# A bidirectional Mamba block with a gated feed-forward layer: the decay ring carried over the chunks, and Silu, evacuations, output products and a norm at other steps

## Chip, cores and metric

The kernel runs on one core of a Trainium2 chip. The metric is the device time of one execution in microseconds (us), the median of a few runs. The core has five engines with queues of their own: PE (TensorE, matrix products), DVE (VectorE), ACT (ScalarE), POOL (GpSimd) and SP, which here only issues DMAs. Each engine takes its instructions strictly in the order in which they are written; engines meet through semaphores.

## The reference

Input x has shape (2, 4096, 256). The network normalises and modulates x, runs a Mamba block over it forwards and backwards in time, joins the two, and adds a feed-forward part. All of the change lies in the Mamba block, whose core is this:

```python
xi = silu(conv(in_proj_x(x)))              # 512 channels, causal convolution over 4 tokens
dt, Bm, Cm = split(xi @ x_proj.T)          # dt: 64 -> 512 channels; B and C: 16 states
dt = softplus(dt @ dt_w.T + dt_b)
dA  = exp(dt[..., None] * A)               # the decay, 512 channels x 16 states
dBx = (dt * xi)[..., None] * Bm[:, :, None, :]
h_t = dA_t * h_(t-1) + dBx_t               # the scan over time
y_t = sum_s(h_t * C_t) + xi * D
out = (y * silu(z)) @ out_proj.T           # z is the other half of in_proj
```

## The kernel before

**Tiling.** Time is cut into chunks of T = 512 tokens. There are 2 passes (backwards, then forwards), 8 chunks per pass and batch entry, and 2 batch entries, which take turns: 32 chunks in all, called chunk 0 to 31 below (0 to 15 are pass 0). Channels lie on the 128 partitions, in KI = 4 groups. A chunk has 16 states x 4 groups = 64 scans of 128x512, the steps 0 to 63. Two steps are a unit: units 0 to 31, each of one state and of two channel groups. `half` 0 is units 0 to 15 and half 1 is units 16 to 31.

**What happens in a step.** ACT computes the decay of step k (`decay`, L885) into one of NDA = 3 banks of PSUM, the decay ring. DVE scans it (`scan`, L1057). POOL multiplies dt*xi by B for both groups of a unit (`weigh_b`, L968) into one of four buffers `dBx`. Four units later the states `h` of a unit are multiplied by C: on DVE for 23 of the 32 units (`D_UNITS`, L1066, with C spread over the partitions by PE, L663), on POOL for 9 (`P_UNITS`, L979). Before that ACT copies the last column of each pair of units as the state for the next chunk (`keep_state`, L829). PE turns the weighed states and sums them in PSUM (L681); after 16 units it adds the skip part (L693) and ACT evacuates the sum (`evacuate`, L849). A chunk ends in gates with silu(z) (DVE, L1045) and the output product (PE, L648), evacuated by ACT with Tanh (L861).

**Order.** Chunk n's scans run beside the front part of chunk n+1 (turn of the normalised x, in_proj, convolution, x_proj, dt, z), the tail of chunk n-1 (last gates, output product) and, in pass 0, the norm of x for chunk n+2. Nothing is scheduled by a program. Tuples by hand say at which step each job starts on PE (`AT`); ACT follows PE's table `ACT_LAG` = 3 steps later, and other tuples name the steps of jobs that are ACT's alone. ACT's body is

```python
for k in range(STEPS):
    decay(ch, k)
    if k == EVAC[1] and has(ch, -1): evacuate(ch.go(-1), 1)
    if k == EVAC[0]: evacuate(ch, 0)
    tail(ch.go(-1), k)
    front(ch.go(1), k); xi_silu(ch.go(1), k)
    z_silu(ch, k)
    scale_skip(ch, k)
    if k % 4 == 2: keep_state(...)         # units (k-6)/2 and (k-6)/2 + 1
    if k == AT_XN and norms(ch, 2): norm_x(ch.go(2))
```

ACT's functions need tables: Silu is in one set, Exp in another, so each group of Silu has an ACT_TABLE_LOAD before it and one behind it, before the next decay. Copies and Identity need no load.

**The decay ring.** `decay(k)` waits until the bank's last user has been scanned. Before the change the banks are fixed per chunk, `SLOT = [k % 3 for k in 0..62] + [1]`: decay k waits for scan k-3, except that decay 63 waits for scan 61 and decay 1 for scan 63 of the chunk before.

Of the kernel before, what the change touches and what calls it, by code (L numbers as in the profile page):

```python
# [22 lines left out]
KI = DI // P  # L23
# [17 lines left out]
AT = {J_LN: (0, 1), J_X: (3, 5, 7, 9), J_CONV: (11, 16, 20, 24), J_DT: (35, 40, 43, 49), J_Z: (50, 52, 54, 56),  # L41
      J_Y: (46, 47, 13, 17), J_OUT: (33, 39)}
AT_LN, AT_X, AT_CONV, AT_DT, AT_Z, AT_Y, AT_OUT = (AT[j] for j in (J_LN, J_X, J_CONV, J_DT, J_Z, J_Y, J_OUT))
# [9 lines left out]
NDA = 3  # L53
SLOT = [k % NDA for k in range(STEPS - 1)] + [1]
NH, NDBX = 8, 4
# [4 lines left out]
ACT_LAG, DVE_LAG = 3, 2  # L60
EVAC = (43, 11)
AT_XI, AT_ZS = (24, 24, 31, 31), (20, 20, 62, 62)
AT_XN = 27
AT_EXP = (48, 53)
AT_LNP = (49, 54)
NORM_STAT, NORM_AGGR, RSTD_S = 6, 7, 11
AT_XD = (14, 15, 16, 18)
# [7 lines left out]
RAW_ROWS = 128  # L75


def since_slot(k):

    return next(n for n in range(1, STEPS) if SLOT[(k - n) % STEPS] == SLOT[k])  # L80

# [242 lines left out]
def mamba(nc, a, bank, ident, cols, mod, norm_c, x_v, yb_v, yf_v, xn_v, b_dram, c_dram, w_raw, s_raw, S):  # L324
# [10 lines left out]
    with ExitStack() as c:  # L335
# [219 lines left out]
        def _(pe):  # L555
# [15 lines left out]
            def front(ch, g):  # L571
# [10 lines left out]
                for m in range(KI):  # L582
# [27 lines left out]
                    if g == AT_B + m:  # L610

                        pe.wait_ge(S["xi"], ch.at(KI, m + 1))
                        part(ch, J_B, m, KI, w_x[:, m, :], xi[:, m, :], B0 + 2 * DS)
# [120 lines left out]
        def _(act):  # L734
# [70 lines left out]
            def xi_silu(ch, g):  # L805
                for m in range(KI):
                    if g == AT_XI[m]:
                        if m == 0:

                            wait(act, S["u_ready"], ch.at(2, 0))  # L810
                        wait_drained(act, ch, J_CONV[m])
                        act.activation(xi[:, m, :], u[:, ch.batch, m, :], ACT.Silu).then_inc(S["xi"], 1)

            def scale_skip(ch, g):
                for m in range(KI):
                    if g == AT_XD[m]:
                        if m == 0:
                            act.wait_ge(S["xi"], ch.at(KI, KI))
                            act.sem_inc(S["go"], 1)
                            wait(act, S["y_turned"], ch.at(2, 0))  # L820
                        col = COL_D + m
                        act.activation(xD[:, m, :], xi[:, m, :], ACT.Copy, scale=cols[:, ch.ps, col:col + 1]
                                       ).then_inc(S["skip"], 1)
# [8 lines left out]
            def z_silu(ch, g):  # L832
                for m in range(KI):
                    if g == AT_ZS[m]:
                        wait_drained(act, ch, J_Z[m])
                        o = z[:, ch.batch, m, :]
                        act.activation(o, o, ACT.Silu).then_inc(S["z"], 1)
# [38 lines left out]
            def decay(ch, k):  # L876
# [148 lines left out]
        def _(dve):  # L1025
# [502 lines left out]
```

## Time and profile before

| | us |
|---|---|
| median of 3 runs (lowest, highest) | 5023.15 (5022.44, 5025.08) |
| the profiled execution | 5024.78, with a span of 5023.0 |
| busy over the span: PE, DVE | 4351.3, 4014.6 |
| busy over the span: ACT, POOL | 3278.4, 3469.0 |

The span is what the core's instructions take; the 1.8 us more of the profiled execution lie around it. The scans run from 156.7 to 3608.2 us of the span, the feed-forward part after that. In the profile a row of a timeline gives the start, the length, the engine, the line, the operation and how many like it follow each other; behind it in brackets stands the idle time of the engine before it, and what ended that.

### The profile page before, as it was taken

To read this page: it belongs to the slowest core of one execution; us is meant where nothing else is said; L and a number is where in the kernel's file an instruction comes from. 1 tells how busy PE (TensorE), PEld (TensorE's weight loads), DVE (VectorE), ACT (ScalarE), POOL (GpSimd) and SP (SyncE) were. 2 spreads that over 40 slices of the span, in tenths; PEclk is the share of its full clock that TensorE was granted. 3 is DMA by queue.
4 is the path that set the end of the run, shared out by engine and by line. 5 is a ranking of instruction groups with operands and counts; after the bars stand their busy time and mean duration, and the time that the engine had idled before them with its cause. 6 is when DMAs were issued, how large, how long until landed. Compare 5 with 4: busy or idle time off the path is not lost. (4 is left out here: it accounts for less than half of the span.)

```text
span 5023.0 us, 61527 instructions
## 1 busy us (share of the span) xinstructions
PE 4351.3 (87%) x22474; PEld 3152.1 (63%) x22474; DVE 4014.6 (80%) x4232; ACT 3278.4 (65%) x5347; POOL 3469.0 (69%) x1589
## 2 busy tenths in 40 slices
PE   3788888888888888888888888888679999999999
PEld 2455555555555655555555555655568888888887
DVE  4699999999999999999999999999744444444442
ACT  4777777777777777777777777777434444444443
POOL 4899999999999999999999999999600000000000
PEclk7999999999999999999999999999889999999999
DMA  4533333333333333333333333323231010101000
GB/s 141 196 116 118 112 112 120 117 116 110 110 112 112 123 115 113 117 111 111 115 106 115 112 110 114 111 110 106 75 132 35 28 36 27 37 26 38 26 30 9
DMA packets 175537, 474.42 MB, mean 94 GB/s; under 512 B 14912, under 2 KB 99264, under 8 KB 140608
## 3 DMA queue, kind: packets, MB, share of 16 engines
q1 hardware_dynamic: 174336, 458.92, 26.6%
q10 hardware_dynamic: 896, 11.54, 0.7%
q8 instruction: 179, 2.93, 0.2%
q14 instruction: 126, 1.03, 0.1%
HBM read 434.75 MB, written 47.19 MB: 96 GB/s over the span
## 5 line engine op out<-in xcount | busy, mean ns | idle before, releaser
L968 POOL TENSOR_TENSOR m_dBx<-m_u,m_Bs 128x1024 f32<-128x1024 f32 x1024 | 2398.7, 2369 | 38.6 <-DVE m_h L1057 34.1
L1057 DVE TENSOR_TENSOR_SCAN m_h<-bank,m_state,m_dBx 128x512 f32<-128x512 f32 x1792 | 2185.5, 1264 | 90.9 <-ACT bank L885 87.7
L885 ACT ACTIVATE bank<-m_dt,cols 128x512 f32<-128x512 f32 x2048 | 1382.7, 690 | 514.9 <-DVE m_h L1057 510.9
L681 PEld LDWEIGHTS bank<-ident,m_h 128*128 128x128 f32 x8192 | 1013.3, 147 | 665.2 <-issue 331.8
L681 PE MATMUL bank<-ident,m_h 128*128 128x128 f32 x8192 | 1260.3, 284 | 155.3 <-DVE m_h L1066 134.8
L1066 DVE TENSOR_TENSOR m_h<-m_h,bank 128x1024 f32<-128x1024 f32 x736 | 879.9, 1196 | 12.1 <-PE bank L663 11.3
L663 PEld LDWEIGHTS bank<-ident,m_Ct 128*128 128x128 f32 x2944 | 345.3, 143 | 728.3 <-DVE m_h L1066 521.3
L663 PE MATMUL bank<-ident,m_Ct 128*128 128x128 f32 x2944 | 485.1, 290 | 365.9 <-DVE m_h L1066 364.7
L1339 POOL TENSOR_TENSOR mvj<-mvj,norm_c 128x4 f32<-128x4 f32 x16 | 16.2, 1013 | 1098.8 <-DVE mvj L1389 1098.8
L979 POOL TENSOR_TENSOR m_h<-m_h,m_Cs 128x1024 f32<-128x1024 f32 x288 | 683.0, 2371 | 30.4 <-ACT m_state L829 26.7
L567 PE MATMUL bank<-m_hT,m_w_in 128*128 128x512 f32 x1024 | 549.9, 623 | 12.8 <-ACT m_hT L755 12.8
L567 PE MATMUL bank<-m_xpre,m_diag 128*128 128x512 f32 x1024 | 522.8, 595 | 0.0
L1227 PE MATMUL bank<-gb,h 128*128 128x512 f32 x2048 | 481.6, 396 | 0.0
L1227 PE MATMUL bank<-ga,h 128*128 128x512 f32 x2048 | 480.5, 396 | 0.0
L1227 PEld LDWEIGHTS bank<-ga,h 128*128 128x128 f32 x2048 | 384.7, 188 | 93.1
L1227 PEld LDWEIGHTS bank<-gb,h 128*128 128x128 f32 x2048 | 383.6, 188 | 91.7
L1431 DVE TENSOR_TENSOR ga<-raw,ga 128x512 fp32r<-128x512 f32 x256 | 176.1, 688 | 315.8 <-ACT raw L1299 314.3
L1057 DVE TENSOR_TENSOR_SCAN m_h<-bank,m_dBx 128x512 f32<-128x512 f32 x256 | 297.6, 1205 | 77.6 <-ACT bank L885 69.7
L1431 DVE TENSOR_TENSOR gb<-raw,gb 128x512 fp32r<-128x512 f32 x128 | 88.7, 693 | 245.0 <-ACT raw L1299 245.0
L1297 ACT ACTIVATE gb<-bank,fcol 128x512 fp32r<-128x512 f32 x128 | 88.2, 689 | 291.6 <-PE bank L1227 291.6
L1297 ACT ACTIVATE ga<-bank,fcol 128x512 fp32r<-128x512 f32 x128 | 88.2, 689 | 288.3 <-PE bank L1227 288.3
L648 PE MATMUL bank<-m_w_out,m_z 128*128 128x256 f32 x1024 | 263.8, 381 | 1.9 <-DVE m_z L1045 1.1
(125 smaller groups left out, 4919.8 us busy)
## 6 DMA issues: line engine op xcount, KB each, us to landing
m_Bs<-b_dram SPq DMA_DIRECT2D x256, 1024.0 KB, 4.7
m_Cs<-c_dram SPq DMA_DIRECT2D x288, 256.0 KB, 3.2
m_xy<-in_x SPq DMA_DIRECT2D x16, 512.0 KB, 7.1
xn_dram<-m_xn SPq DMA_DIRECT2D x16, 512.0 KB, 4.5
yb_dram<-m_ysb SPq DMA_DIRECT2D x16, 512.0 KB, 2.9
m_xn<-xn_dram SPq DMA_DIRECT2D x16, 512.0 KB, 3.8
x_dram<-m_ysb SPq DMA_DIRECT2D x16, 512.0 KB, 2.9
x<-x_dram SPq DMA_DIRECT2D x16, 512.0 KB, 5.0
```

Of the source, the lines that this page charges most:

```text
L567: mm = pe.matmul(FB[BANK[i]][0:rows, :], lhsT, rhs, start=(k == 0), stop=(k == kn - 1))
L648: mm = pe.matmul(FB[BANK[J_OUT[i]]][:, (r // 2) * DM:(r // 2 + 1) * DM], z[:, q, k, s * P:(s + 1) * P], w_out[:, k, :], start=(k == 0), st ...
L663: mm = pe.matmul(CB[:, t * P:(t + 1) * P], Ct[:, ch.batch, t, s:s + 1].broadcast_to((P, P)), ident[:, :], start=True, stop=True, is_transp ...
L681: mm = pe.matmul(YB[b][:, o:o + P], h[:, k % NH, m, tok:tok + P], ident[:, :], start=(s == 0 and o == 0), stop=False, is_transpose=True, s ...
L885: act.activation(DA[SLOT[k]][:, :], dt[:, ch.batch, m, :], ACT.Exp, scale=cols[:, ch.ps, col:col + 1]).then_inc(S["da"], 1)
L968: pool.tensor_tensor(dBx[:, k % NDBX, :, :], u[:, ch.batch, m, :], Bs[:, k // BP % 2, k % BP, :].unsqueeze(1).broadcast_to((P, 2, T)), ALU ...
L979: pool.tensor_tensor(o, o, Cs[:, i % 2, :].unsqueeze(1).broadcast_to((P, 2, T)), ALU.mult).then_inc(S["weigh_p"], 1)
L1057: dve.tensor_tensor_scan(h[:, k % NH, m, flip(ch)], DA[SLOT[i]][:, flip(ch)], dBx[:, k % NDBX, m, flip(ch)], initial, ALU.mult, ALU.add).t ...
L1066: dve.tensor_tensor(o, o, CB[:, :].unsqueeze(1).broadcast_to((P, 2, T)), ALU.mult).then_inc(S["weigh_d"], 1)
L1227: return pe.matmul(out, lhsT, rhs, start=start, stop=stop)
L1297: act.activation(dst, bank[b][:, :], func, **args).then_inc(S["hi"], 1)
L1431: dve.tensor_tensor(dst[:, 1], raw[:, j % XR, :], dst[:, 0].bitcast(F32), ALU.subtract).then_inc(S["lo"], 1)
```

## The change

The ring goes on over the chunks: the bank of a decay is its number since the start of the kernel modulo 3, and each decay waits for the scan three before it. Both Silu of xi in a half become one instruction of 128x1024, and so do those of z. The Silu of z for half 0 moves from step 20 to step 5. The evacuations move from steps 43 and 11 to 44 and 12. The output products start on PE at steps 29 and 35 in place of 33 and 39, so their Tanh on ACT come at 35 and 41 in place of 39 and 45. The norm of x is applied on ACT at step 19 in place of 27; its statistics on DVE move from units 6 and 7 to 4 and 5, its four small operations on POOL from unit 11 to 8.

```diff
--- before.py
+++ after.py
@@ -39,7 +39,7 @@
 J_LN, J_X, J_CONV, J_B, J_DT, J_Z = (0, 1), (2, 3, 4, 5), (6, 7, 8, 9), 10, (11, 12, 13, 14), (15, 16, 17, 18)
 J_Y, J_OUT, J_C = (19, 20, 21, 22), (23, 24), 25
 AT = {J_LN: (0, 1), J_X: (3, 5, 7, 9), J_CONV: (11, 16, 20, 24), J_DT: (35, 40, 43, 49), J_Z: (50, 52, 54, 56),
-      J_Y: (46, 47, 13, 17), J_OUT: (33, 39)}
+      J_Y: (46, 47, 13, 17), J_OUT: (29, 35)}
 AT_LN, AT_X, AT_CONV, AT_DT, AT_Z, AT_Y, AT_OUT = (AT[j] for j in (J_LN, J_X, J_CONV, J_DT, J_Z, J_Y, J_OUT))
 AT_B, AT_C = 29, 37
 NFB = 2
@@ -51,19 +51,18 @@
 
 
 NDA = 3
-SLOT = [k % NDA for k in range(STEPS - 1)] + [1]
 NH, NDBX = 8, 4
 W_LAG, T_LAG = 4, 5
 P_UNITS = (1, 5, 7, 9, 13, 15, 17, 21, 25)
 D_UNITS = tuple(k for k in range(NU) if k not in P_UNITS)
 ND, NP = len(D_UNITS), len(P_UNITS)
 ACT_LAG, DVE_LAG = 3, 2
-EVAC = (43, 11)
-AT_XI, AT_ZS = (24, 24, 31, 31), (20, 20, 62, 62)
-AT_XN = 27
+EVAC = (44, 12)
+AT_XI, AT_ZS = (24, 31), (5, 62)
+AT_XN = 19
 AT_EXP = (48, 53)
 AT_LNP = (49, 54)
-NORM_STAT, NORM_AGGR, RSTD_S = 6, 7, 11
+NORM_STAT, NORM_AGGR, RSTD_S = 4, 5, 8
 AT_XD = (14, 15, 16, 18)
 ADD_S = (27, 2)
 U_S = (31, 6)
@@ -73,11 +72,6 @@
 FFN_WEIGHTS = ("w1T", "w2T", "h1T", "h2T", "w3T")
 PIECE, RING = 2 * DH, 4
 RAW_ROWS = 128
-
-
-def since_slot(k):
-
-    return next(n for n in range(1, STEPS) if SLOT[(k - n) % STEPS] == SLOT[k])
 
 
 class Chunk:
@@ -609,7 +603,7 @@
                         part(ch, J_Z[m], k, KM, w_in[:, k, (KI + m) * P:(KI + m + 1) * P], hT[:, k, :])
                     if g == AT_B + m:
 
-                        pe.wait_ge(S["xi"], ch.at(KI, m + 1))
+                        pe.wait_ge(S["xi"], ch.at(2, m // 2 + 1))
                         part(ch, J_B, m, KI, w_x[:, m, :], xi[:, m, :], B0 + 2 * DS)
                 if g == AT_C:
                     rows = B0 + 2 * DS
@@ -803,19 +797,21 @@
                         act.activation(dt[:, q, m, :], FB[b][:, :], ACT.Relu, bias=bias).then_inc(drain[b], 1)
 
             def xi_silu(ch, g):
-                for m in range(KI):
-                    if g == AT_XI[m]:
-                        if m == 0:
+                for half in range(2):
+                    if g == AT_XI[half]:
+                        if half == 0:
 
                             wait(act, S["u_ready"], ch.at(2, 0))
-                        wait_drained(act, ch, J_CONV[m])
-                        act.activation(xi[:, m, :], u[:, ch.batch, m, :], ACT.Silu).then_inc(S["xi"], 1)
+                        m = 2 * half
+                        for i in (m, m + 1):
+                            wait_drained(act, ch, J_CONV[i])
+                        act.activation(xi[:, m:m + 2, :], u[:, ch.batch, m:m + 2, :], ACT.Silu).then_inc(S["xi"], 1)
 
             def scale_skip(ch, g):
                 for m in range(KI):
                     if g == AT_XD[m]:
                         if m == 0:
-                            act.wait_ge(S["xi"], ch.at(KI, KI))
+                            act.wait_ge(S["xi"], ch.at(2, 2))
                             act.sem_inc(S["go"], 1)
                             wait(act, S["y_turned"], ch.at(2, 0))
                         col = COL_D + m
@@ -830,10 +826,12 @@
                          ).then_inc(S["save"], 1)
 
             def z_silu(ch, g):
-                for m in range(KI):
-                    if g == AT_ZS[m]:
-                        wait_drained(act, ch, J_Z[m])
-                        o = z[:, ch.batch, m, :]
+                for half in range(2):
+                    if g == AT_ZS[half]:
+                        m = 2 * half
+                        for i in (m, m + 1):
+                            wait_drained(act, ch, J_Z[i])
+                        o = z[:, ch.batch, m:m + 2, :]
                         act.activation(o, o, ACT.Silu).then_inc(S["z"], 1)
 
             def evacuate(ch, half):
@@ -879,10 +877,10 @@
                 half, s = divmod(j, DS)
                 if s == 0 and m == 0:
                     act.wait_ge(S["dt_done"], ch.at(2, half + 1))
-                wait(act, S["scan"], ch.at(STEPS, k - since_slot(k) + 1))
+                wait(act, S["scan"], ch.at(STEPS, k - NDA + 1))
                 m += 2 * half
                 col = COL_A + m * DS + s
-                act.activation(DA[SLOT[k]][:, :], dt[:, ch.batch, m, :], ACT.Exp, scale=cols[:, ch.ps, col:col + 1]
+                act.activation(DA[ch.at(STEPS, k) % NDA][:, :], dt[:, ch.batch, m, :], ACT.Exp, scale=cols[:, ch.ps, col:col + 1]
                                ).then_inc(S["da"], 1)
 
 
@@ -1040,7 +1038,7 @@
             def gate(ch, g, m):
                 q = ch.batch
                 if g == AT_Y[m] + DVE_LAG:
-                    dve.wait_ge(S["z"], ch.at(KI, m + 1))
+                    dve.wait_ge(S["z"], ch.at(2, m // 2 + 1))
                     wait_filled(dve, ch, J_Y[m])
                     dve.tensor_tensor(z[:, q, m, :], FB[BANK[J_Y[m]]][:, :], z[:, q, m, :], ALU.mult
                                       ).then_inc(drain[BANK[J_Y[m]]], 1)
@@ -1054,7 +1052,7 @@
                     dve.wait_ge(S["dbx"], ch.at(NU, k + 1))
                 dve.wait_ge(S["da"], ch.at(STEPS, i + 1))
                 initial = 0.0 if ch.opens() else state[:, q, k, m:m + 1]
-                dve.tensor_tensor_scan(h[:, k % NH, m, flip(ch)], DA[SLOT[i]][:, flip(ch)], dBx[:, k % NDBX, m, flip(ch)],
+                dve.tensor_tensor_scan(h[:, k % NH, m, flip(ch)], DA[ch.at(STEPS, i) % NDA][:, flip(ch)], dBx[:, k % NDBX, m, flip(ch)],
                                        initial, ALU.mult, ALU.add).then_inc(S["scan"], 1)
 
             def weigh_c(ch, k):
```

Rows of the program's order, chunk 1 of pass 0. In the changed kernel the line of the decays is L883 (L885 before), of `keep_state` L825 (L829), of Silu of z L835 (L837), of Silu of xi L808 (L812), of the evacuation L847 (L849), of the Tanh L859 (L861). ACT before, from decay 63 to step 6 of the next chunk:

```order
L885 ACTIVATE bank<-m_dt,cols 128x512 x4
L829 COPY m_state<-m_h 128x4
L885 ACTIVATE bank<-m_dt,cols 128x512
L755 ACTIVATE m_hT<-bank,mod 128x512
L885 ACTIVATE bank<-m_dt,cols 128x512
L755 ACTIVATE m_hT<-bank,mod 128x512
L885 ACTIVATE bank<-m_dt,cols 128x512 x2
L829 COPY m_state<-m_h 128x4
```

ACT in the changed kernel at the same place:

```order
L883 ACTIVATE bank<-m_dt,cols 128x512 x4
L825 COPY m_state<-m_h 128x4
L883 ACTIVATE bank<-m_dt,cols 128x512
L749 ACTIVATE m_hT<-bank,mod 128x512
L883 ACTIVATE bank<-m_dt,cols 128x512
L749 ACTIVATE m_hT<-bank,mod 128x512
L883 ACTIVATE bank<-m_dt,cols 128x512
L835 ACT_TABLE_LOAD
L835 ACTIVATE m_z<-m_z 128x1024
L883 ACT_TABLE_LOAD
L883 ACTIVATE bank<-m_dt,cols 128x512
L825 COPY m_state<-m_h 128x4
```

Between decay 5 and decay 6 there are now two table loads and a Silu, and the copy of states of step 6 (the last row) stands behind them.

ACT before, from decay 19 to the Silu of xi and the load behind it (the norm of x, L873, comes after decay 27, five rows further on):

```order
L885 ACTIVATE bank<-m_dt,cols 128x512 x2
L837 ACT_TABLE_LOAD
L837 ACTIVATE m_z<-m_z 128x512 x2
L885 ACT_TABLE_LOAD
L885 ACTIVATE bank<-m_dt,cols 128x512 x2
L778 ACTIVATE m_u<-bank,cols 128x512
L829 COPY m_state<-m_h 128x4
L885 ACTIVATE bank<-m_dt,cols 128x512 x2
L812 ACT_TABLE_LOAD
L812 ACTIVATE m_xi<-m_u 128x512 x2
L885 ACT_TABLE_LOAD
```

ACT in the changed kernel, from step 19 (L871 is the norm of x) to step 26:

```order
L883 ACTIVATE bank<-m_dt,cols 128x512
L871 ACTIVATE m_xn<-m_xy,m_mv 128x256 x4
L883 ACTIVATE bank<-m_dt,cols 128x512 x3
L772 ACTIVATE m_u<-bank,cols 128x512
L825 COPY m_state<-m_h 128x4
L883 ACTIVATE bank<-m_dt,cols 128x512 x2
L808 ACT_TABLE_LOAD
L808 ACTIVATE m_xi<-m_u 128x1024
L883 ACT_TABLE_LOAD
L883 ACTIVATE bank<-m_dt,cols 128x512 x2
```

The Silu of z with its two loads is gone from here, and the norm stands four decays ahead of the Silu of xi instead of behind it.

PE before, in units 15 and 16. L567 with w_x is the product of xi with x_proj, L663 the spread of C for DVE, L681 the turn of states:

```order
L663 MATMUL bank<-ident,m_Ct 128x128 x4
L681 MATMUL bank<-ident,m_h 128x128 x4
L567 MATMUL bank<-m_xi,m_w_x 96x512
L681 MATMUL bank<-ident,m_h 128x128 x4
L567 MATMUL bank<-m_xi,m_w_x 96x512
L663 MATMUL bank<-ident,m_Ct 128x128 x4
L681 MATMUL bank<-ident,m_h 128x128 x4
L567 MATMUL bank<-m_xi,m_w_x 96x512
L681 MATMUL bank<-ident,m_h 128x128 x4
L648 MATMUL bank<-m_w_out,m_z 128x256 x2
```

PE in the changed kernel at the same place (L642 is the output product, L561, L657 and L675 are L567, L663 and L681 of before):

```order
L657 MATMUL bank<-ident,m_Ct 128x128 x4
L675 MATMUL bank<-ident,m_h 128x128 x4
L642 MATMUL bank<-m_w_out,m_z 128x256 x2
L561 MATMUL bank<-m_xi,m_w_x 96x512
L675 MATMUL bank<-ident,m_h 128x128 x4
L642 MATMUL bank<-m_w_out,m_z 128x256 x2
L561 MATMUL bank<-m_xi,m_w_x 96x512
L657 MATMUL bank<-ident,m_Ct 128x128 x4
L675 MATMUL bank<-ident,m_h 128x128 x4
L642 MATMUL bank<-m_w_out,m_z 128x256 x2
L561 MATMUL bank<-m_xi,m_w_x 96x512
```

Three groups of the output product, each two matrix products of 128x256, now stand among the last three of x_proj; a fourth stands with the first of x_proj in unit 14. The last three groups of the other output product leave units 19 to 21 in the same way, and end in unit 19.

## Rows read from the trace of the kernel before

**Rows 1.** Waits of DVE over the span: who for whom, us in total, times, longest

```profile
DVE m_h L1057 <- ACT bank L885: 157.4, 97, 56.4
```

**Rows 2.** Timeline of DVE, scan 63 of chunks 1, 13, 17 and 31

```profile
366.19 1.22 DVE L1057 TENSOR_TENSOR_SCAN m_h<-bank,m_dBx 128x512 f32<-128x512 f32 x1 [0.84 <-ACT bank L885]
...
1676.94 1.28 DVE L1057 TENSOR_TENSOR_SCAN m_h<-bank,m_state,m_dBx 128x512 f32<-128x512 f32 x1 [0.66 <-ACT bank L885]
...
2106.41 1.22 DVE L1057 TENSOR_TENSOR_SCAN m_h<-bank,m_dBx 128x512 f32<-128x512 f32 x1 [0.84 <-ACT bank L885]
...
3608.16 1.28 DVE L1057 TENSOR_TENSOR_SCAN m_h<-bank,m_state,m_dBx 128x512 f32<-128x512 f32 x1 [0.66 <-ACT bank L885]
```

**Rows 3.** Timeline of DVE within chunk 6

```profile
843.19 1.20 DVE L1066 TENSOR_TENSOR m_h<-m_h,bank 128x1024 f32<-128x1024 f32 x1
844.30 3.63 DVE L1057 TENSOR_TENSOR_SCAN m_h<-bank,m_state,m_dBx 128x512 f32<-128x512 f32 x3
848.96 1.28 DVE L1057 TENSOR_TENSOR_SCAN m_h<-bank,m_state,m_dBx 128x512 f32<-128x512 f32 x1 [1.03 <-ACT bank L885]
...
879.72 2.46 DVE L1057 TENSOR_TENSOR_SCAN m_h<-bank,m_state,m_dBx 128x512 f32<-128x512 f32 x2 [1.53 <-ACT bank L885]
...
896.49 1.22 DVE L1066 TENSOR_TENSOR m_h<-m_h,bank 128x1024 f32<-128x1024 f32 x1 [0.32 <-PE bank L663]
```

**Rows 4.** Timeline of ACT around step 62 of chunk 5, and steps 5 and 6

```profile
797.84 0.69 ACT L885 ACTIVATE bank<-m_dt,cols 128x512 f32<-128x512 f32 x1 [0.48 <-DVE m_h L1057]
798.55 1.28 ACT L837 ACT_TABLE_LOAD   x1
799.85 1.15 ACT L837 ACTIVATE m_z<-m_z 128x512 f32<-128x512 f32 x2
...
802.40 1.30 ACT L885 ACTIVATE bank<-m_dt,cols 128x512 f32<-128x512 f32 x2
...
810.60 1.49 ACT L885 ACTIVATE bank<-m_dt,cols 128x512 f32<-128x512 f32 x2
812.03 0.18 ACT L829 COPY m_state<-m_h 128x4 f32<-128x4 f32 x1
```

**Rows 5.** Timeline of ACT, steps 25, 43, 44 and 48 of chunk 6

```profile
848.24 1.30 ACT L885 ACTIVATE bank<-m_dt,cols 128x512 f32<-128x512 f32 x2
...
876.76 1.07 ACT L849 COPY m_acc<-bank 128x512 f32<-128x512 f32 x2 [2.50 <-PE bank L693]
...
878.88 1.32 ACT L885 ACTIVATE bank<-m_dt,cols 128x512 f32<-128x512 f32 x2
...
885.08 1.06 ACT L746 ACTIVATE m_u<-m_u 128x1024 f32<-128x1024 f32 x1
```

**Rows 6.** Timeline of POOL: same instruction of chunks 2 and 3, and chunk 6

```profile
362.42 2.37 POOL L957 TENSOR_TENSOR m_u<-m_dt,m_xi 128x1024 f32<-128x1024 f32 x1
...
468.90 2.35 POOL L957 TENSOR_TENSOR m_u<-m_dt,m_xi 128x1024 f32<-128x1024 f32 x1
...
813.76 2.38 POOL L979 TENSOR_TENSOR m_h<-m_h,m_Cs 128x1024 f32<-128x1024 f32 x1
...
872.38 9.32 POOL L968 TENSOR_TENSOR m_dBx<-m_u,m_Bs 128x1024 f32<-128x1024 f32 x4
```

**Rows 7.** Timeline of PE, units 15, 16 and 25 of chunk 6

```profile
857.24 0.65 PE L663 MATMUL bank<-ident,m_Ct 128*128 128x128 f32 x4 [0.79 <-DVE m_h L1066]
...
860.72 0.65 PE L663 MATMUL bank<-ident,m_Ct 128*128 128x128 f32 x4 [0.24 <-DVE m_h L1066]
...
862.94 1.03 PE L648 MATMUL bank<-m_w_out,m_z 128*128 128x256 f32 x4
...
891.50 1.12 PE L681 MATMUL bank<-ident,m_h 128*128 128x128 f32 x4 [1.78 <-DVE m_h L1066]
892.41 1.92 PE L567 MATMUL bank<-m_hT,m_w_in 128*128 128x512 f32 x2
```

**Rows 8.** Windows: length, busy PE, PE loads, DVE, ACT, POOL, granted clock, DMA, GB/s

```profile
892.20:895.60 3.40, 3.40 (x10) 1.91 (x10) 3.40 (x4) 2.93 (x4) 3.40 (x2) 0.61 0.58 241
```

## The prediction

> **What bounds the kernel now.** I read the waits of DVE first, then the timeline of DVE over whole chunks, then at each wait the timeline of the engine named. Over the span DVE waits 157.4 us for decays from ACT, in 97 waits [rows 1]; 56.4 of it is one wait, the start. The other 101 us are what matters: 96 waits, three per chunk. Scan 63 comes again after (1676.94 - 366.19) / 12 = 109.23 us in chunks 2 to 13 and after (3608.16 - 2106.41) / 14 = 107.27 us in chunks 18 to 31 [rows 2]. Within a chunk the waits stand at the same four places [rows 2, 3]: 1.03 us before scan 25, 1.53 before scan 44, 0.66 before scan 63, all for ACT, and 0.32 for PE before one weighing. That is 3.54 us per chunk; the rest, 105.7 us in pass 0, is DVE's own work. So DVE bounds the Mamba part, and ACT makes it wait three times per chunk.
>
> POOL is close behind. Between one instruction of chunk 2 and the same of chunk 3 lie 106.48 us [rows 6], a stretch in which POOL waits for nobody. In pass 1 it has no norm: four of its large products take 9.32 us and one 2.37 [rows 6], so (9.32 - 2.37) / 3 = 2.32 start to start, and the 45 of a chunk (32 with B, 9 with C, 4 around dt) 104.4 us. No chunk can be faster than that.
>
> **How a group of Silu is covered.** ACT may run three scans ahead. Decay k starts when scan k-3 ends; decay k+1 must be there when scan k ends. Between the two, DVE has three scans (1.18 each, start to start), and one or two weighings of 1.11 [rows 3]: 4.65 or 5.76 us. ACT has two decays of 0.69, two loads of 1.28 and the Silu. As two instructions the Silu take 1.15 [rows 4]; for one of 128x1024 the nearest row is the Exp of that shape, 1.06 [rows 5]. The chain is 5.0 us. With one weighing it is some 0.3 us too long, with two it is hidden with 0.7 to spare.
>
> **The change, part by part (us per chunk).**
>
> *Silu of z, from step 20 to 5.* Before, ACT comes out of this group without a pause and falls into that of xi at step 24; decay 25 starts at 848.24 and ends at 848.93, while DVE was ready at 844.30 + 3.63 = 847.93 [rows 3, 5]. Without the group at step 20, decay 24 can start when scan 21 ends, at 843.2 [rows 3]. Only one weighing lies in the cover, so decay 25 ends at 843.2 + 5.0 = 848.2 and 0.3 of the wait stays: gain 0.7. At its new place two weighings lie in the cover. Decay 5 started at 810.60 [rows 4], so decay 6 ends at 815.6, against 810.6 + 5.76 = 816.3 when it is wanted: cost nothing, hidden by DVE's weighings of the units before. What stands behind it is the copy of states of step 6, below.
>
> *Evacuation, from 43 to 44.* ACT waits 2.50 us for PE's sum, evacuates at 876.76, then has a pair of dt left, and starts decay 44 only at 878.88 [rows 5]; DVE waits 1.53 [rows 3]. Now the pair of dt and decay 44 (two instructions of dt and one decay, each about 0.69) fit into the 2.50 us of waiting ahead of the evacuation. Decay 45 ends at 876.76 + 1.07 + 0.69 = 878.5, and is wanted one scan after 878.2, at 879.4. Gain 1.53, all of it. Bound: if the dt product comes late from PE, half of that, 0.8.
>
> *Pairs.* 0.1 less at step 62: decay 62 starts at 797.84, decay 63 at 802.40 [rows 4]. One weighing is in its cover, so the wait goes from 0.66 to 0.56: gain 0.1. The ring changes decays 63 and 1 alone. Decay 63 is held up by ACT's own queue there, not by scan 61, so the third bank buys nothing: 0, hidden behind the Silu.
>
> *Norm of x from 27 to 19 (chunks 0 to 13).* Four instructions of 128x256, each shorter than a decay of 128x512, so under 2.8 us. With decays around it 0.69 + 2.8 + 0.69 = 4.2 us, under the 4.65 of cover: 0. The statistics on DVE keep their length. POOL's part is now asked for earlier, and can make POOL wait a little at unit 8, but DVE does not ask for those products yet.
>
> *Output products from 33 and 39 to 29 and 35.* Each group is four records of 1.03 us, 0.87 start to start [rows 7]. Unit 15 starts at 857.24, unit 16 at 860.72 after 0.24 idle [rows 7]: 3.24 us of work, which two more groups make 5.0. The next spread then starts at 862.3 and takes 0.65; DVE wants it two scans after the weighing that released 860.72, at about 863.0. The margin is about zero. I take a new wait of 0.1, between 0 and 0.5. The wait of 0.32 stays.
>
> **The sum.** 0.7 + 1.53 + 0.1 = 2.33 per chunk. Chunks 2 to 13: 12 x 2.33 = 28.0, to 106.90 per chunk, just above POOL's 106.48. Chunk 14: 2.3. In chunks 15 to 17 POOL has to build new weights for the convolution and is the bound; 3 us for all three, between 0 and 7. Chunks 18 to 30: 13 x 2.33 = 30.3, to 104.94, above POOL's 104.4. Chunks 0 and 1 are fed by POOL, and chunk 31 has no Silu of xi beside it: 0. Together 63.6, less 26 x 0.1 for PE: 61.0. The feed-forward part doesn't change. The profiled execution (5024.78) would be at 4963.8; the median of the runs is 1.6 lower, so 5023.15 - 61.0 = 4962.
>
> **Rivals.**
>
> *DVE waits for nobody (0.12).* If the group at 24, that at 62 and PE fit after all, POOL is the bound: 12 x (109.23 - 106.48) = 33, 13 x (107.27 - 104.4) = 37, and 6 for the rest: 76 us, 4947. For it speaks that the sum above already ends within half a microsecond of POOL. Against it, the chain of 5.0 is longer than its cover of 4.65.
>
> *PE is late (0.22).* Either in units 15 to 18 by up to 0.5, or in units 25 and 26. There the groups for z took 1.92 us per pair of records in place of 1.02, after 1.78 us of idleness [rows 7]. The granted clock was 0.61 over this stretch [rows 8], so at the 1.2 GHz level for most of it, and that made the 0.32 us. The output products leave units 19 to 21, so there is more idleness ahead of it. Two groups at the low clock are up to 1.0 more. Price 0.5 to 1.0 on 25 chunks, 12 to 25 us: 4974 to 4987. The Trainium skill (TensorE: Matmul & The Clock Gate, "What's actually happening") has the clock at half after idleness; by that the trace agrees.
>
> *POOL is held behind the Silu of z (0.04), no change.* POOL's product at 813.76 needs the copy of states of step 6, at 812.03 before [rows 4, 6], now at 815.8. POOL waits 2.0 us or more, up to 2.6. If that were exposed whole, a chunk would be 106.48 + 2.6 = 109.1 in pass 0 and 104.4 + 2.6 = 107.0 in pass 1: 12 x 0.1 + 13 x 0.3 = 5 us less than now, 5018. It is exposed once POOL hands over the products of unit 22 too late: they were ready at 872.38 + 2.33 = 874.7, and DVE would ask at 879.72 - 1.53 - 0.7 = 877.5. The 2.8 us between cover the 2.6, so I expect DVE not to feel it; but it is the thinnest cover.
>
> *PE at the low clock in units 14 to 16 (0.03), slower.* Unit 15 has 5.0 us of PE work now, and no margin. If the 0.8 to 1.1 us of idleness ahead of it brought the clock down, as 1.78 us did in unit 25, its 5.0 us would double, all of it in DVE's way: 5.0 - 2.33 = 2.7 more per chunk, 25 x 2.7 = 67, 5090. It decides from 2.33 us of new wait on. Against it: the product of unit 16 takes 1.03 us [rows 7], the speed of the 2.4 GHz level, after this same idleness.
>
> *A dearer table switch (0.01).* A group at step 5 with 2.8 us more in its chain (7.8 against 5.76) would cost 2.0 per chunk: 5012. In the rows a load is followed by its Silu 0.02 us after its end [rows 4], and nothing more is lost. The Trainium skill (ScalarE: Activation LUTs, "What ACT_TABLE_LOAD costs") adds a drain of 1.38 us to each load of 1.28; no row here shows it.
>
> **How the numbers follow.** The forecast has 0.58: 4962, by its own bounds (evacuation 0.8 in place of 1.53, PE 0 to 0.3, chunks 15 to 17) 4953 to 4972. The range of 8 in 10 takes in DVE waiting for nobody and PE late: 4944 to 4988. A measurement of this kernel can tell 0.2%, 10 us. Faster by more: 0.58 + 0.12 + 0.22 + 0.01 = 0.93; within: 0.04; slower: 0.03.
>
> **What would show it.** Scan 63 of chunks 1 and 13 some 12 x 106.9 = 1283 us apart, not 1311; DVE's wait before scan 44 gone, before scan 25 some 0.3, before scan 63 some 0.55, and none before scan 6; a new wait of POOL's product with C (unit 5) for the copy of states, 0.5 us or more; the weighing in unit 16 waiting for PE 0.1 or not at all. Wrong: a wait of DVE for dBx in units 20 to 26, for PE of over 0.5 in units 15 to 18, or PE's clock low in more of a chunk.

## The result and the profile after

| | before | changed |
|---|---|---|
| median (lowest, highest) | 5023.29 (5022.44, 5025.08) | 4973.75 (4972.42, 4975.22) |
| profiled execution, its span | 5024.78, 5023.0 | 4973.31, 4971.5 |

The ratio is 0.9901, 95% interval 0.9884 to 0.9918: 49.5 us less, 1.0%. The forecast was 61 less. The two profiled executions differ by 51.5, since the one before lay 1.5 above its median.

Timeline of DVE in the changed kernel, scan 63 of chunks 1, 13, 17 and 31, which answers to [rows 2]:

```profile
365.55 1.22 DVE L1055 TENSOR_TENSOR_SCAN m_h<-bank,m_dBx 128x512 f32<-128x512 f32 x1 [0.74 <-ACT bank L883]
...
1652.36 1.28 DVE L1055 TENSOR_TENSOR_SCAN m_h<-bank,m_state,m_dBx 128x512 f32<-128x512 f32 x1 [0.57 <-ACT bank L883]
...
2078.30 1.23 DVE L1055 TENSOR_TENSOR_SCAN m_h<-bank,m_dBx 128x512 f32<-128x512 f32 x1 [0.75 <-ACT bank L883]
...
3556.86 1.28 DVE L1055 TENSOR_TENSOR_SCAN m_h<-bank,m_state,m_dBx 128x512 f32<-128x512 f32 x1 [0.56 <-ACT bank L883]
```

The differences between these rows and those of [rows 2] place the gain. Up to chunk 1 it is 0.6 us. Chunks 2 to 13 took 1310.75 and now take 1286.81: 23.9 less, 107.23 per chunk. Chunks 14 to 17 gave 3.5, chunks 18 to 31 took 1501.75 and now 1478.56: 23.2 less, 105.61 per chunk. Together 51.3 at the last scan; the feed-forward part is as long as before.

Next, what DVE waits for. The chief rows of its waits over chunks 2 to 13 (who for whom, us in total, times, longest), in the kernel before:

```profile
DVE m_h L1057 <- ACT bank L885: 39.5, 37, 1.5
DVE m_h L1066 <- PE bank L663: 3.9, 12, 0.4
```

and in the changed kernel:

```profile
DVE m_h L1055 <- ACT bank L883: 13.2, 25, 0.7
DVE m_h L1064 <- PE bank L657: 6.8, 16, 0.5
```

Before, DVE waits three times per chunk for ACT; now twice. 26.3 us of these waits went in twelve chunks, and 2.9 us came back as waits for PE. In chunks 18 to 31 the same two rows are, before:

```profile
DVE m_h L1057 <- ACT bank L885: 43.4, 41, 1.5
DVE m_h L1066 <- PE bank L663: 2.1, 6, 0.4
```

and in the changed kernel:

```profile
DVE m_h L1055 <- ACT bank L883: 14.8, 28, 0.7
DVE m_h L1064 <- PE bank L657: 9.2, 13, 1.3
```

Here 28.6 went and 7.1 came back, with a longest wait of 1.3 that was not there before.

Within chunk 6, the timeline of DVE in the changed kernel, which answers to [rows 3]:

```profile
831.59 2.44 DVE L1055 TENSOR_TENSOR_SCAN m_h<-bank,m_state,m_dBx 128x512 f32<-128x512 f32 x2
...
839.16 1.28 DVE L1055 TENSOR_TENSOR_SCAN m_h<-bank,m_state,m_dBx 128x512 f32<-128x512 f32 x1 [0.48 <-ACT bank L883]
...
864.82 1.19 DVE L1064 TENSOR_TENSOR m_h<-m_h,bank 128x1024 f32<-128x1024 f32 x1
865.93 4.80 DVE L1055 TENSOR_TENSOR_SCAN m_h<-bank,m_state,m_dBx 128x512 f32<-128x512 f32 x4
871.20 1.22 DVE L1064 TENSOR_TENSOR m_h<-m_h,bank 128x1024 f32<-128x1024 f32 x1 [0.47 <-PE bank L657]
...
901.44 1.28 DVE L1055 TENSOR_TENSOR_SCAN m_h<-bank,m_state,m_dBx 128x512 f32<-128x512 f32 x1 [0.56 <-ACT bank L883]
```

Scan 25 waits 0.48 (before 1.03), scan 44 lies within the x4 at 865.93 and does not wait (before 1.53), scan 63 waits 0.56 (before 0.66). The weighing in unit 26 waits 0.38 (before 0.32) in this chunk, but the trace has this wait in only 4 of chunks 2 to 13, where before all 12 had it, and in none of 18 to 31, where before 5 had it. New is the 0.47 at 871.20: the weighing of unit 18, which comes in unit 22, two scans behind the place where the 1.53 was. It stands in every chunk from 3 to 14 and from 18 to 30. What is late there is PE. Its timeline in the changed kernel:

```profile
865.85 1.04 PE L687 MATMUL bank<-ident,m_xD 128*128 128x128 f32 x8
868.36 1.09 PE L675 MATMUL bank<-ident,m_h 128*128 128x128 f32 x8 [1.47 <-ACT m_acc L847]
869.39 1.12 PE L561 MATMUL bank<-m_dbB,m_w_dt 64*128 64x512 f32 x2
870.44 0.65 PE L657 MATMUL bank<-ident,m_Ct 128*128 128x128 f32 x4
```

PE has finished the sum of a half (L687), and cannot begin the next one until ACT has evacuated it; behind the turns stand a dt product and only then the spread of C (L657) that the weighing needs. ACT at that time:

```profile
866.62 0.69 ACT L883 ACTIVATE bank<-m_dt,cols 128x512 f32<-128x512 f32 x1
867.23 1.07 ACT L847 COPY m_acc<-bank 128x512 f32<-128x512 f32 x2
```

The evacuation comes right behind decay 44 and waits for nobody: the sum was there first. So the chain sum, evacuation, turns, dt product, spread is what DVE now waits for.

POOL's wait for the copy of states came at the place that was foretold, and in the steady part DVE did not feel it: in chunks 2 to 13 it waits for `dBx` once, for 0.2 us. Timeline of POOL, changed kernel, chunk 6, unit 5:

```profile
806.54 2.36 POOL L977 TENSOR_TENSOR m_h<-m_h,m_Cs 128x1024 f32<-128x1024 f32 x1 [0.72 <-ACT m_state L825]
```

It is shorter than the 2.0 to 2.6 that the prediction gave it, and it is no added wait: before, the same wait stood later in the chunk, at the product of unit 21 (1.01 us at 882.71 of chunk 6), and over the span such waits were 26.7 us in 36 times; now they are 21.5 in 20, the longest 1.6.

### The profile page after: what moved, and what is told of

Read it like the earlier page. It is cut to its first block and busy times, and to the rows that moved or that the text cites. A ratio compares the mean times of both kernels' runs of the same rounds, so it can differ in the third digit from the quotient of the medians.

```text
span 4971.5 us, 61496 instructions
## 1 busy us (share of the span) xinstructions
PE 4328.7 (87%) x22474; PEld 3147.1 (63%) x22474; DVE 4010.0 (81%) x4232; ACT 3270.6 (66%) x5219; POOL 3463.4 (70%) x1589
## 3 DMA queue, kind: packets, MB, share of 16 engines
q14 instruction: 126, 1.03, 0.1%
## 5 line engine op out<-in xcount | busy, mean ns | idle before, releaser
L883 ACT ACTIVATE bank<-m_dt,cols 128x512 f32<-128x512 f32 x2048 | 1380.3, 688 | 469.3 <-DVE m_h L1055 462.9
L675 PEld LDWEIGHTS bank<-ident,m_h 128*128 128x128 f32 x8192 | 1008.6, 147 | 656.2 <-issue 328.0
L675 PE MATMUL bank<-ident,m_h 128*128 128x128 f32 x8192 | 1244.9, 284 | 170.8 <-DVE m_h L1064 109.6
L657 PEld LDWEIGHTS bank<-ident,m_Ct 128*128 128x128 f32 x2944 | 344.2, 143 | 683.6 <-DVE m_h L1064 471.1
L657 PE MATMUL bank<-ident,m_Ct 128*128 128x128 f32 x2944 | 486.2, 290 | 320.7 <-DVE m_h L1064 318.5
L977 POOL TENSOR_TENSOR m_h<-m_h,m_Cs 128x1024 f32<-128x1024 f32 x288 | 683.1, 2372 | 21.6 <-ACT m_state L825 21.5
L561 PE MATMUL bank<-m_hT,m_w_in 128*128 128x512 f32 x1024 | 543.1, 616 | 15.0 <-ACT m_hT L749 12.8
L561 PE MATMUL bank<-m_xpre,m_diag 128*128 128x512 f32 x1024 | 522.6, 594 | 0.0
L642 PE MATMUL bank<-m_w_out,m_z 128*128 128x256 f32 x1024 | 262.6, 380 | 1.9 <-DVE m_z L1043 1.1
```

The costliest lines, as they stand in the source:

```text
L561: mm = pe.matmul(FB[BANK[i]][0:rows, :], lhsT, rhs, start=(k == 0), stop=(k == kn - 1))
L642: mm = pe.matmul(FB[BANK[J_OUT[i]]][:, (r // 2) * DM:(r // 2 + 1) * DM], z[:, q, k, s * P:(s + 1) * P], w_out[:, k, :], start=(k == 0), st ...
L657: mm = pe.matmul(CB[:, t * P:(t + 1) * P], Ct[:, ch.batch, t, s:s + 1].broadcast_to((P, P)), ident[:, :], start=True, stop=True, is_transp ...
L675: mm = pe.matmul(YB[b][:, o:o + P], h[:, k % NH, m, tok:tok + P], ident[:, :], start=(s == 0 and o == 0), stop=False, is_transpose=True, s ...
L883: act.activation(DA[ch.at(STEPS, k) % NDA][:, :], dt[:, ch.batch, m, :], ACT.Exp, scale=cols[:, ch.ps, col:col + 1]).then_inc(S["da"], 1)
L977: pool.tensor_tensor(o, o, Cs[:, i % 2, :].unsqueeze(1).broadcast_to((P, 2, T)), ALU.mult).then_inc(S["weigh_p"], 1)
```

## The experiments

Each kernel was timed beside the kernel before; every ratio is to that one.

### What each part is worth, taken from the changed kernel

**The evacuations put back.**

```diff
-EVAC = (44, 12)
+EVAC = (43, 11)
```

> The changed kernel with the evacuations back at steps 43 and 11. Theory (DVE's waits, place by place): the evacuation at 44 took away the wait before scan 44 (1.5 us) but brought a wait of 0.47 for PE at the weighing of unit 18, since PE now waits 1.5 us for the evacuation. Back at 43, the first returns at about 1.5 and the second goes: 1.0 us more in some 27 chunks, 27 us, about 5000. Rival (POOL is the bound after the change, and what DVE waits for elsewhere costs nothing): 0 to 5 us more, about 4976.

Measured 4998.94, ratio 0.9951 (0.9938 to 0.9965). Its timelines of DVE and ACT:

```profile
869.18 1.19 DVE L1064 TENSOR_TENSOR m_h<-m_h,bank 128x1024 f32<-128x1024 f32 x1
...
874.23 2.46 DVE L1055 TENSOR_TENSOR_SCAN m_h<-bank,m_state,m_dBx 128x512 f32<-128x512 f32 x2 [1.50 <-ACT bank L883]
```

```profile
871.28 1.07 ACT L847 COPY m_acc<-bank 128x512 f32<-128x512 f32 x2 [1.94 <-PE bank L687]
```

The wait of 1.50 is back before scan 44 and the one of 0.47 is gone: while DVE stands still for ACT, PE catches up. 1.50 - 0.47 = 1.03 per chunk over some 25 chunks is close to the 25.2 us that the kernel takes more than the changed one. The row of ACT also shows how late the evacuation has become: here, where it waits for the sum itself, it starts 871.28 - 869.18 = 2.10 behind the weighing before it; in the changed kernel 867.23 - 864.82 = 2.41. Some 0.3 of the new 0.47 is the evacuation behind decay 44, the rest is PE's chain.

**The output products put back.**

```diff
-      J_Y: (46, 47, 13, 17), J_OUT: (29, 35)}
+      J_Y: (46, 47, 13, 17), J_OUT: (33, 39)}
```

> The changed kernel with the output products back at steps 33 and 39. Theory: they make the sum of half 0 and the spread of unit 18 0.9 us later on PE in units 20 and 21; the wait at the weighing of unit 18 grows from 0.47 to about 0.9: 0.4 us in 27 chunks, 4984; PE has more slack in units 15 to 18, which gives nothing. Rival: the crowding of units 15 to 18 costs more than it saves: 4970 or faster.

Measured 4994.18, ratio 0.9942 (0.9929 to 0.9956): 20.4 us more than the changed kernel, not 10. Timeline of its DVE:

```profile
875.20 1.22 DVE L1064 TENSOR_TENSOR m_h<-m_h,bank 128x1024 f32<-128x1024 f32 x1 [1.36 <-PE bank L657]
```

and of its PE:

```profile
871.50 0.66 PE L675 MATMUL bank<-ident,m_h 128*128 128x128 f32 x4 [0.61 <-ACT m_acc L847]
871.99 1.03 PE L642 MATMUL bank<-m_w_out,m_z 128*128 128x256 f32 x4
...
873.38 1.12 PE L561 MATMUL bank<-m_dbB,m_w_dt 64*128 64x512 f32 x2
874.44 0.65 PE L657 MATMUL bank<-ident,m_Ct 128*128 128x128 f32 x4
```

A group of the output product (L642) stands between the evacuation and the spread. From the end of the evacuation to the spread PE has 874.44 - 871.50 = 2.94 of work; in the changed kernel 870.44 - 868.36 = 2.08. The 0.86 more is this one group, and the wait is 1.36 in place of 0.47, 0.89 more. Over 25 chunks that is 22 us.

**The Silu of z of half 0 put back.**

```diff
-AT_XI, AT_ZS = (24, 31), (5, 62)
+AT_XI, AT_ZS = (24, 31), (20, 62)
```

> The changed kernel with the first group of Silu of z back at step 20 (in pairs, the norm still at 19). Theory: ACT has the norm, this group and that of xi behind one another; in pass 0 decay 25 comes 2.7 us late in place of 0.5, in pass 1 1.0 late: 12 x 2.2 + 14 x 0.5 = 33, about 5007, and POOL's wait for the copy of states in unit 5 goes. Rival (the wait of POOL in unit 5 behind the Silu at step 5 is what ate the missing gain): 4974 or faster.

Measured 4999.07, ratio 0.995 (0.9937 to 0.9964), 25.3 more than the changed kernel, where 33 were expected. Its DVE in chunk 6:

```profile
842.88 1.28 DVE L1055 TENSOR_TENSOR_SCAN m_h<-bank,m_state,m_dBx 128x512 f32<-128x512 f32 x1 [1.28 <-ACT bank L883]
...
849.76 1.28 DVE L1055 TENSOR_TENSOR_SCAN m_h<-bank,m_state,m_dBx 128x512 f32<-128x512 f32 x1 [0.94 <-ACT bank L883]
```

and its ACT:

```profile
835.84 2.06 ACT L871 ACTIVATE m_xn<-m_xy,m_mv 128x256 f32<-128x256 f32 x4
...
838.49 1.28 ACT L835 ACT_TABLE_LOAD   x1
```

Two waits stand where the changed kernel has one. Before scan 25 it is 0.94, so the move takes 0.94 - 0.48 = 0.46 off this wait, in both passes. The 1.28 before scan 21 is another thing: the norm, now at step 19, and the Silu at step 20 have one decay between them, and run into each other. That happens only in pass 0, where there is a norm. So by its waits the move of the Silu is worth 0.46 x 25 = 11.5 us by itself, and the rest goes with what it spares the moved norm, 1.28 in each of some 12 chunks. By the distances between scans 63 this kernel takes 24.4 us more than the changed one in chunks 2 to 13, with the norm, and 3.7 in chunks 18 to 31, without it. The waits for ACT there grew by the expected 5.9 us (20.7 against 14.8), but those for PE were 1.7 shorter (7.5 against 9.2).

**The ring, the norm and the pairs.** Three kernels: the ring fixed per chunk again (with its wait), the norm back at its old steps, and each pair of Silu written as two instructions at the new places. The first and the third edit are shown in part: the table of the banks, the wait on it and the scan's bank come back too, and the pair of xi is split in the same way.

```diff
-DA[ch.at(STEPS, k) % NDA][:, :]
+DA[SLOT[k]][:, :]
```

```diff
-AT_XN = 19
+AT_XN = 27
-NORM_STAT, NORM_AGGR, RSTD_S = 4, 5, 8
+NORM_STAT, NORM_AGGR, RSTD_S = 6, 7, 11
```

```diff
-                        act.activation(o, o, ACT.Silu).then_inc(S["z"], 1)
+                        act.activation(o, o, ACT.Silu)
+                        act.activation(o2, o2, ACT.Silu).then_inc(S["z"], 1)
```

> The changed kernel with the banks of the decays fixed per chunk again (decay 63 waits for scan 61, decay 1 for scan 63 of the chunk before). Theory: decay 63 stands behind a group of Silu on ACT, so the ring buys nothing: 4974, within 2 us. Rival: the group of Silu at step 5 needs all the lead that ACT can get ahead of it, and decay 1 half a microsecond later is passed on: 0.6 us in 28 chunks, 4990.

Measured 4975.11, ratio 0.9905 (0.9889 to 0.992): no difference that can be told from the changed kernel.

> The changed kernel with only the norm of x put back (ACT at step 27, DVE units 6 and 7, POOL unit 11). Theory: the norm's place is hidden in either kernel, no more than one chunk's start feels it: 4974, within 3 us of the changed kernel. Rival: at step 27 its four instructions stand right behind the Silu of xi and delay the decays there, on 14 chunks, by 0.3 us or more: 4978 or above. Other rival: at step 19 it costs something that the forecast missed: 4970 or below.

Measured 4973.37, ratio 0.9898 (0.9882 to 0.9914): none either.

> The changed kernel with every pair of Silu written as two instructions of 128x512 again, at the same places. Theory: the two groups with one weighing in their cover (steps 24 and 62) become 0.09 us longer each, 25 chunks x 0.18 = 4.5 us: 4978. Rival: a pair saves nothing that DVE feels, 4974. Other rival: two semaphore releases or a second access setup count for more, 4984 and above.

Measured 4980.4, ratio 0.9913 (0.9899 to 0.9927). The median is 6.6 more and lies between the theory (4978) and the second rival (4984); the intervals overlap, so the difference is not shown by the times. The profiles show some of it: in chunk 6 scan 25 waits 0.57 in place of 0.48 and scan 63 0.66 in place of 0.56, and the last scan starts at 3560.98, 4.1 us later.

### The two edits around step 44, from the side of the kernel before

**The evacuations alone moved to 44 and 12, in the kernel before.**

```diff
-EVAC = (43, 11)
+EVAC = (44, 12)
```

> The kernel before with only the evacuations moved to steps 44 and 12. Theory: the wait of 1.53 before scan 44 goes, and since the output product still stands in units 20 and 21 on PE, the weighing of unit 18 waits 0.8: 0.7 us in 26 chunks, 18 us, about 5005. If the evacuation alone carries most of the change: 1.5 in 26 chunks, 4983.

Measured 5018.77, ratio 0.9991 (0.9982 to 1.0): 4.3 us less by the medians, between 0 and 9 by the interval, where 18 were expected. The theory of that run missed. Its DVE:

```profile
879.59 1.22 DVE L1066 TENSOR_TENSOR m_h<-m_h,bank 128x1024 f32<-128x1024 f32 x1 [1.36 <-PE bank L663]
```

The wait of 1.53 for ACT is gone, and 1.36 for PE has come in its place two scans later, the same 1.36 as with the output products put back above. Nearly all of the gain is given back: 1.53 - 1.36 = 0.17 per chunk is left, 4.3 us over 25 chunks. In the kernel before, the PE row of that spread and the DVE row of the weighing that needs it are:

```profile
880.83 0.65 PE L663 MATMUL bank<-ident,m_Ct 128*128 128x128 f32 x4
```

```profile
882.09 1.19 DVE L1066 TENSOR_TENSOR m_h<-m_h,bank 128x1024 f32<-128x1024 f32 x1
```

There the spread ended at 881.48, 0.6 us before DVE began the weighing. Half of these 0.6 go because the evacuation now stands behind decay 44: it starts 2.44 us behind the weighing ahead of it, before 2.14.

**The output products alone moved, and both together, in the kernel before.** The first has this edit alone, the second also that of the evacuations.

```diff
-      J_Y: (46, 47, 13, 17), J_OUT: (33, 39)}
+      J_Y: (46, 47, 13, 17), J_OUT: (29, 35)}
```

> The kernel before with only the output products on PE moved to 29 and 35. Theory: they pay only when the evacuation comes behind decay 44, since before that DVE waits 1.53 us for ACT at scan 44 whatever PE does: 5023, within 4 us of before. Rival, both edits add up: 20 us less, since that is what the changed kernel lost when they were put back: 5003.

Measured 5023.9, ratio 1.0001 (0.9991 to 1.001): nothing. The wait before scan 44 is 1.50.

> The kernel before with the evacuations at 44 and 12 and the output products at 29 and 35. Theory, the two pay together: the wait of 1.53 before scan 44 goes and 0.5 us for PE at the weighing of unit 18 comes in its place, about 1.0 us on 25 chunks: 4999. Rival, the evacuation alone is all that counts, as it was without the other: 5019. In between, 5008, if another wait takes over.

Measured 4991.52, ratio 0.9934 (0.992 to 0.9948): 32 us. Its waits of DVE in chunks 2 to 13:

```profile
DVE m_h L1057 <- ACT bank L885: 21.1, 25, 1.0
DVE m_h L1066 <- PE bank L663: 8.9, 16, 1.1
```

One edit gives 4, the other nothing, and the two 32. Before, DVE's wait for ACT hid a chain on PE that ended only 0.6 us ahead of it. With only one of the two made shorter, the other sets the end.

### The waits that are left

**The Silu of z of half 1 at step 63, where two weighings cover it.**

```diff
-AT_XI, AT_ZS = (24, 31), (5, 62)
+AT_XI, AT_ZS = (24, 31), (5, 63)
```

> The changed kernel with the second group of Silu of z at step 63 in place of 62. Theory: what covers a group is the DVE work between scan k-3 and scan k+1; behind an even step of the end of a chunk it holds one weighing (4.65 us), behind step 63 two (5.8 us), over the chain of 5.1. The wait of 0.56 before scan 63 goes; 0.56 in 27 chunks less what POOL's own time takes back in pass 0: 13 to 15 us, 4959 to 4961. Rival (POOL is the bound): 4974.

Measured 4956.09, ratio 0.9867 (0.9852 to 0.9882). The wait before scan 63 is gone in every chunk of the steady part. Its ACT and DVE around that place:

```profile
895.23 1.28 ACT L835 ACT_TABLE_LOAD   x1
896.52 1.06 ACT L835 ACTIVATE m_z<-m_z 128x1024 f32<-128x1024 f32 x1
897.60 1.28 ACT L883 ACT_TABLE_LOAD   x1
```

```profile
895.58 1.19 DVE L1064 TENSOR_TENSOR m_h<-m_h,bank 128x1024 f32<-128x1024 f32 x1
896.69 2.45 DVE L1055 TENSOR_TENSOR_SCAN m_h<-bank,m_state,m_dBx 128x512 f32<-128x512 f32 x2
899.06 1.19 DVE L1064 TENSOR_TENSOR m_h<-m_h,bank 128x1024 f32<-128x1024 f32 x1
```

The two loads and the Silu between them now lie beside two weighings and two scans with no idle time. That is the rule of cover in its purest form: one step later, nothing else changed, 17.7 us less than the changed kernel. It is somewhat more than the 13 to 15 expected: that sum counted 27 chunks, but in the changed kernel this wait stands in all 32, 18.7 us together, and here in none.

**The third dt product of PE one step later, behind the spread.**

```diff
-AT = {..., J_DT: (35, 40, 43, 49), ...}
+AT = {..., J_DT: (35, 40, 44, 49), ...}
```

> The changed kernel with the third dt product on PE at step 44 in place of 43, so behind the spread of unit 18 and not ahead of it. Theory: the spread comes 1.0 us earlier, and the wait of 0.47 at the weighing of unit 18 goes: 12 us, 4962. Rival (the wait comes from elsewhere or POOL is the bound): 4974, or slower if the dt pair, one step later on ACT, holds up the turn of y at step 46.

Measured 4959.55, ratio 0.9874 (0.9859 to 0.9889), 14.2 less than the changed kernel. Its PE:

```profile
866.95 1.09 PE L675 MATMUL bank<-ident,m_h 128*128 128x128 f32 x8 [1.48 <-ACT m_acc L847]
867.88 0.60 PE L657 MATMUL bank<-ident,m_Ct 128*128 128x128 f32 x4
...
868.84 1.12 PE L561 MATMUL bank<-m_dbB,m_w_dt 64*128 64x512 f32 x2
```

PE still waits 1.48 for the evacuation, but the spread now comes 0.93 behind the turns instead of 2.08, and the weighing doesn't wait: the trace has no wait at this place in any chunk. The 14.2 are more than the 12 expected because some of these waits had been longer than 0.47 (see the last section).

**Both.**

> The Silu of z at step 63 and the third dt product at step 44 together. Theory: 1.03 us less per chunk for DVE; POOL's own 106.48 limits pass 0 to 0.75, in pass 1 1.0 is had: 12 x 0.75 + 14 x 1.0 = 23, 4951. Rival (POOL bound already): 4974.

Measured 4949.35 (4948.9 to 4954.77), ratio 0.9857 (0.9842 to 0.9872). It is the fastest of all, 74 us below before and 24 below the changed kernel. The two alone gave 17.7 and 14.2, together 24.4 and not 31.9. In chunks 18 to 31 the two add up: 6.9 and 6.3 alone, 14.4 together, by the distances between scans 63. In chunks 2 to 13 they don't: 6.3 and 5.7 alone, 7.6 together. And chunks 15 to 17 take 322.5 us, 2.6 more than in the changed kernel. These two stretches are where POOL is full. In chunks 15 to 17 it is busy for 322.1 of the 322.5 us. In chunks 2 to 13 its row reads (window, length, busy POOL and instructions, granted clock, DMA share, GB/s):

```profile
363.64:1642.86 1279.22, 1274.81 (x589) 0.96 0.35 118
```

POOL waits for nobody there, and now and then DVE waits for it. Timeline of DVE, chunks 6, 7 and 13:

```profile
835.83 1.28 DVE L1055 TENSOR_TENSOR_SCAN m_h<-bank,m_state,m_dBx 128x512 f32<-128x512 f32 x1 [0.48 <-ACT bank L883]
...
972.14 2.46 DVE L1055 TENSOR_TENSOR_SCAN m_h<-bank,m_state,m_dBx 128x512 f32<-128x512 f32 x2 [0.64 <-POOL m_dBx L966]
...
1581.69 1.28 DVE L1055 TENSOR_TENSOR_SCAN m_h<-bank,m_state,m_dBx 128x512 f32<-128x512 f32 x1 [0.48 <-ACT bank L883]
```

From scan 25 of chunk 6 to that of chunk 13 it is (1581.69 - 835.83) / 7 = 106.55 us per chunk, against the 106.48 that POOL itself needs [rows 6]. Why POOL's work in chunks 15 to 17 took 2.6 us longer was not traced.

## Why the prediction was right, and where it was off

**What bounds the kernel: right.** The time followed DVE's waits. The floor by POOL was real as well: the fastest kernel stands on it at 106.55, and its 4949.35 is close to the 4947 of the rival "DVE waits for nobody". That rival's title doesn't hold, though: DVE still waits there, 0.48 before scan 25 in nearly every chunk, while POOL sets the pace.

**The forecast and its bounds.** The measured 4973.75 lies 12 us above the forecast and just above its "own bounds" of 4953 to 4972. Those bounds were added up wrongly: the evacuation at 0.8 in place of 1.53 is 0.73 x 25 = 18 us by itself, and alone would give 4980. The 12 us are at the lower edge of the rival "PE is late" (4974 to 4987). What happened is that rival in kind, a new wait for PE, but neither at its places (units 15 to 18, or 25 and 26) nor by its means (crowding there, or the low clock): in most chunks it comes at the full granted clock.

**Silu of z, 0.7 forecast, 0.55 measured.** The mechanism was right, and the size off: the chain of 5.0 is 5.13. DVE had ended scan 21 at 831.59 + 2.44 = 834.03 and started scan 25 at 839.16. The 0.13 are the hand-overs between the engines and 0.01 to 0.02 between each two instructions of ACT, which the sum of durations leaves out. With a cover of 4.65 the wait is 0.48, not 0.3. Of the 0.55, 0.09 is the pair and 0.46 the move. At step 5 the group cost nothing, as forecast, and no wait stands before scan 6 in the steady part. Chunk 0, which was not in the sum, has one of 2.19 there.

**Pairs, 0.1 forecast.** Before scan 63 the wait fell from 0.66 to 0.56. The Trainium skill (ScalarE: Activation LUTs, "What ACT_TABLE_LOAD costs") gives an activation without a pointer operand a fixed part of 186 ns, of which 93 ns overlap with the one before; as an estimate from these figures, a pair in one instruction saves 93 ns. The trace agrees: 1.15 us as two [rows 4], 1.06 as one.

**Evacuation, 1.53 forecast, "all of it".** Here the step failed in what it left out. ACT's side was right: scan 44 doesn't wait, and the two instructions of dt and a decay fit into ACT's wait for the sum. But the prediction followed only ACT's queue. PE cannot start the next half before the evacuation, and the weighing of unit 18 needs PE's spread behind it. The prediction looked for a new wait of 0.1 in unit 16, at the added output products; there is none there (the weighing at 853.16 follows a scan without a pause), and the one in unit 22 is 0.47. The worth of the move was booked as 1.53 x 25 = 38 us; putting it back in the changed kernel cost 25.2. The size of the whole error on PE's side: in chunks 18 to 31 waits for PE grew by 7.1 us where 1.3 were forecast, in chunks 2 to 13 by 2.9 where 1.2 were. The new wait alone is larger, 9.2 and 5.3; the wait in unit 26, which was forecast to stay, mostly went.

**Output products, forecast as a cost of 0.1.** In truth they are the condition of the gain. Without their move, 0.86 us more stand between the evacuation and the spread, and the evacuation alone brings 4 us, while both together bring 32. That the sum came near is in part luck: the gain was booked wholly under the evacuation, as if PE had no part in it, and by the same reasoning the evacuation alone would have been forecast at 38 us.

**Ring and norm, 0 each: right.** One remark: the norm's move costs nothing only because the Silu of z left step 20. With both at 19 and 20, scan 21 waits 1.28 in pass 0. That is the cover of 4.65 again, against one chain of norm, decay, loads and Silu.

**The sum.** Forecast per stretch against measured: chunks 2 to 13 26.8 and 23.9, chunk 14 2.2 and 1.2, chunks 15 to 17 3 and 2.3, chunks 18 to 31 29.0 and 23.2. Waits for ACT that stayed longer than forecast make 3.4 of the 8.7 us missing in the two long stretches (28.0 - 26.3 and 30.3 - 28.6), waits for PE 7.5; what remains is -2.2. DVE's own busy time is 1.4 and 1.7 us shorter in the two stretches (1266.77 against 1268.15, 1454.98 against 1456.69), which covers it; why it is shorter was not traced. One sign that the prediction had called wrong did appear, in chunks 15 to 17: DVE waits 0.94 to 1.26 us for `dBx` in unit 22. The prediction had put just these chunks at POOL's pace.

## What to carry to other kernels

Before you book a removed wait as gain, look at every engine that used that wait to catch up: here a wait of 1.53 us on one queue hid a chain on another that ended 0.6 us earlier, and one edit was worth 4 us, the other 0, and the two 32. For each switch of tables, count what lies beside it on the other engine between the two hand-overs, in instructions, and add a tenth of a microsecond for the hand-overs; moving it by one step can be worth 0.5 us per pass through the loop. Find the next engine's floor early: here it told both where further tuning ends and why two gains of 18 and 14 us made 24.

## What was not expected of the hardware

After the same idle time TensorE's clock fell in one chunk and not in another. In the changed kernel PE waits 1.47 us for the evacuation in chunk 6 and in chunk 27, with the same instructions of PE around it. In chunk 27, of pass 1, the timeline of PE then reads:

```profile
3101.83 1.09 PE L675 MATMUL bank<-ident,m_h 128*128 128x128 f32 x8 [1.47 <-ACT m_acc L847]
3102.85 1.41 PE L561 MATMUL bank<-m_dbB,m_w_dt 64*128 64x512 f32 x2
3104.19 1.11 PE L657 MATMUL bank<-ident,m_Ct 128*128 128x128 f32 x4
```

where chunk 6 had 1.12 and 0.65 for the last two. In the changed kernel, windows of PE over the two places (length, busy PE, granted clock, DMA share, GB/s):

```profile
3102.80:3105.20 2.40, 2.40 (x9) 0.66 1.00 198
...
869.30:871.20 1.90, 1.90 (x11) 1.00 0.86 172
```

A granted clock of 0.66 means that most of that stretch ran at the 1.2 GHz level; in chunk 6 it was 2.4 GHz throughout. The weighing there, at 3105.41, waits 1.21 us in place of 0.47. What decides between the two no run here shows. So the same wait is dear in some chunks: of chunks 18 to 30, four (22, 24, 27 and 30) have 1.20 to 1.29 at this weighing and nine 0.46 or 0.47. Over the 3 us ahead of it the granted clock is 0.67 to 0.69 in the four and 1.00 in the nine. The four make some 3.1 us of the 9.2 of waits for PE in chunks 18 to 31. Nor are they tied to the chunk: with the evacuations and output products moved in the kernel before, it is chunks 6, 9, 12 and 14 that have 1.0 to 1.1.
